# Attention in front of a recurrence and two mixtures: TensorE's groups in another order, PSUM banks allotted anew, key copies placed one by one

## The reference, cut to what matters

```
q = layernorm(x) @ Wq.T + bq         # 16 heads of 16 values
k = ctx @ Wk.T + bk ;  v = ctx @ Wv.T + bv
attn = softmax(q k^T / 4) over the 361 rows of ctx
x = x + tanh(g) * ((attn v) @ Wo.T + bo)
```

## Time and profile before

| | |
|---|---|
| median of three runs | 3206.34 us |
| the profiled execution | 3209.85 us |
| its span, from the first to the last instruction | 3208.1 us |
| busy over the span | PE 90%, DVE 41%, ACT 26%, POOL 25% |
| granted TensorE clock, mean over the span | 0.953 |

### The profile page before, as it was taken

One profiled execution on the slowest core, in us unless ns is written; L12 is line 12 of the kernel. 1 busy time (PEld: TensorE's weight loads), 2 busy tenths in 40 slices (PEclk: granted clock), 3 DMA queues, 4 the chain that ended last, 5 costly groups with the idle time before them and its releaser, 6 DMA issues. The chain is left out here.

```text
span 3208.1 us, 70894 instructions
## 1 busy us (share of the span) xinstructions
PE 2880.4 (90%) x29244; PEld 1559.8 (49%) x29245; DVE 1310.6 (41%) x2655; ACT 827.8 (26%) x2170; POOL 811.1 (25%) x759
## 2 busy tenths in 40 slices
PE   7999999899999999999999999999999974009898
PEld 4566666534444444444444444478566643007555
DVE  5655555613332323323323233264222256986311
ACT  3444444411111111111111111121222246471111
POOL 2111111002222222222222222234444431004243
PEclk9999999999999999999999999999999988559899
DMA  7000100220000000000000000051222263005143
GB/s 239 30 26 26 32 26 26 71 81 23 18 23 18 19 22 18 23 17 21 19 18 25 16 24 16 18 205 47 43 45 45 44 175 98 0 1 206 52 116 75
DMA packets 78391, 164.11 MB, mean 51 GB/s; under 512 B 11788, under 2 KB 51568, under 8 KB 73111
## 3 DMA queue, kind: packets, MB, share of 16 engines
q1 hardware_dynamic: 53588, 104.04, 10.4%
q0 software_dynamic: 21456, 40.57, 5.7%
q10 hardware_dynamic: 3074, 15.45, 1.3%
HBM read 119.63 MB, written 40.37 MB: 50 GB/s over the span
## 5 line engine op out<-in xcount | busy, mean ns | idle before, releaser
L1076 PE MATMUL gru_ps_rz<-whh,scratch 128*32 128x512 f32 x6400 | 709.3, 595 | 0.0
L871 POOL TENSOR_TENSOR scratch<-scratch 128x1024 f32<-128x1024 f32 (+3 forms) x246 | 369.5, 1527 | 818.8 <-DVE stat L885 656.5
L1076 PEld LDWEIGHTS gru_ps_rz<-whh,scratch 128*32 128x32 f32 x6400 | 197.9, 110 | 454.1 <-issue 454.1
L1081 PE MATMUL gru_ps_n<-whh,scratch 128*32 128x256 f32 x6400 | 363.6, 379 | 0.0
L1005 DVE TENSOR_TENSOR scratch<-scratch,state 128x256 f32<-128x256 f32 x100 | 52.2, 522 | 667.4 <-ACT scratch L1034 667.4
L1081 PEld LDWEIGHTS gru_ps_n<-whh,scratch 128*32 128x32 f32 x6400 | 207.7, 110 | 180.2 <-issue 59.9
L467 DVE TENSOR_REDUCE att_neg_max<-att_banks 100x2 f32<-100x722 f32 x256 | 221.1, 906 | 122.6 <-PE att_banks L701 122.6
L1034 ACT ACTIVATE scratch<-gru_ps_rz 128x512 f32<-128x512 f32 x100 | 59.7, 597 | 726.7 <-PE gru_ps_rz L1076 726.7
L390 ACT ACTIVATE att_probsT<-att_banks 121x600 f32<-121x600 f32 x256 | 154.3, 672 | 216.7 <-PE att_banks L744 216.7
L1053 PE MATMUL gru_ps_rz<-wih,scratch 128*32 128x512 f32 x1600 | 191.7, 597 | 1.7 <-POOL scratch L973 1.7
L2392 PE MATMUL e_ps_g<-align_reach,ident 32*121 32x101 f32 x64 | 10.9, 326 | 197.0 <-DVE align_reach L2198 195.5
(11 more groups left out here) (400 smaller groups left out, 4237.8 us busy)
## 6 DMA issues: line engine op xcount, KB each, us to landing
table<-in_w SPq DMA_DIRECT2D x16, 1024.0 KB, 6.9
states<-state SPq DMA_DIRECT2D x100, 128.0 KB
scratch<-states SPq DMA_DIRECT2D x25, 512.0 KB, 3.5
whh<-in_whhT POOLq DMA_DIRECT2D x8, 1536.0 KB, 19.9
att_c_in<-in_ctxT SPq DMA_DIRECT2D x32, 363.0 KB, 3.2
dist_ctx<-in_ctxT SPq DMA_DIRECT2D x32, 363.0 KB, 4.6
align_ctx<-in_ctx_rows SPq DMA_DIRECT2D x32, 363.0 KB
whh<-in_guT ACTq DMA_DIRECT2D x8, 1024.0 KB, 12.3
```

The source lines that it names most:

```text
L871: done = nc.gpsimd.tensor_tensor(last.prod[:, row:row + rows, :], a, b, ALU.mult)
L1076: last = nc.tensor.matmul(ps_rz[quarter(q), :], stateT[c % 2][:, quarter(c // 2)], rz_columns(whh, c, q), start=False, stop=(c == GC - 1))
L1081: last = nc.tensor.matmul(ps_n[quarter(q), 0:GQ], stateT[c % 2][:, quarter(c // 2)], n_columns(whh, c, q), start=(c == 0), stop=(c == GC - 1))
```

## The change

The change alters the order of the calls on TensorE, ScalarE and VectorE, gives each tensor other PSUM banks and rewrites the waits that guard them. `keys_out` copies one half at a time, so that its calls can stand apart. The instructions themselves and their count stay. Shown are the bank tables, the three loops and the waits that the prediction speaks of.

```diff
-        SCORES = ((4, 0), (6, 4), (4, 2), (4, 0))
-        TURNED = ((0, 2), (6, 2), (4, 0), (2, 0))
-        OUTPUTS, XT, QUERIES, BACK, ATT, Y, MAXIMA = 6, 7, 0, 6, 1, 2, 5
-        KEYS, VALUES, V_ORDER = (7, 3), (7, 7, 3), (0, 2, 1)
+        SCORES = ((4, 6), (4, 1), (2, 0), (1, 6))
+        TURNED = ((2, 0), (6, 2), (1, 6), (2, 0))
+        OUTPUTS, XT, QUERIES, BACK, ATT, Y, MAXIMA = 4, 4, 5, 3, 4, 4, 7
+        KEYS, VALUES, V_ORDER = (0, 3), (1, 6, 5), (0, 2, 1)
...
             for i in range(-3, B + 1):          # ScalarE
+                here, after, later, before = valid(i), valid(i + 1), valid(i + 2), valid(i - 1)
-                if valid(i): exponential(i, 0, 0), exponential(i, 0, 1)
-                if i % 2 and valid(i + 3): xnT_out((i + 3) // 2)
-                if valid(i - 1): att_out(i - 1)
+                if before: att_out(i - 1)
                 if i == B: roots(EARLY, B - 1, 2)
-                if valid(i + 1): keys_out(i + 1, 1)
-                if valid(i + 3): queries_out(i + 3)
-                if valid(i): exponential(i, 1, 0), (i, 1, 1), (i, 2, 0), (i, 2, 1)
-                if valid(i - 1): attnT_out(i - 1)
-                if valid(i + 2): keys_out(i + 2, 0)
+                if here: exponential(i, 0, 0), exponential(i, 0, 1)
+                if after: keys_out(i + 1, 1, 0), keys_out(i + 1, 1, 1)
+                if later: keys_out(i + 2, 0, 0)
+                if here: exponential(i, 1, 1), exponential(i, 1, 0)
+                if i % 2 and valid(i + 3): xnT_out((i + 3) // 2)
+                if later: keys_out(i + 2, 0, 1)
+                if here: exponential(i, 2, 0)
+                if valid(i + 3): queries_out(i + 3)
+                if before: attnT_out(i - 1)
+                if here: exponential(i, 2, 1)
                 if i == AT_ROOT: input_roots()
                 if i == EARLY + 1: roots(0, EARLY, 1)
-                if valid(i): exponential(i, 3, 1), exponential(i, 3, 0)
+                if here: exponential(i, 3, 0), exponential(i, 3, 1)
...
             for i in range(-3, B):              # VectorE
+                early_output(i, 0)
+                if 0 <= i < AT_ROOT: input_statistics(i, 0)
                 if after: maxima(i + 1, 0, 0), maxima(i + 1, 0, 1)
-                if after: maxima(i + 1, 1, 0), maxima(i + 1, 1, 1)
-                early_output(i, 0)
-                if 0 <= i < AT_ROOT: input_statistics(i, 0)
+                if after: maxima(i + 1, 1, 1), maxima(i + 1, 1, 0), values_out(i + 1, 0)
                 if before: divide(i - 1)
-                if after: maxima(i + 1, 2, 1), maxima(i + 1, 2, 0)
+                if after: maxima(i + 1, 2, 0), maxima(i + 1, 2, 1)
+                if before: add_output(i - 1)
                 if 0 <= i < AT_ROOT: input_statistics(i, 1)
-                if after: values_out(i + 1, 0), maxima(i + 1, 3, 0), maxima(i + 1, 3, 1)
-                if before: add_output(i - 1)
-                if after: values_out(i + 1, 2), take_maxima(i + 1)
-                if before: statistics(i - 1), aggregate(i - 1)
+                if after: maxima(i + 1, 3, 0), maxima(i + 1, 3, 1), values_out(i + 1, 2)
+                if before: statistics(i - 1), aggregate(i - 1)
+                if after: take_maxima(i + 1)
...
             for i in range(-3, B + 1):          # TensorE
+                if before: outputs(i - 1, 3)
                 if here: scores_less_maxima(i, 0)
-                if before: outputs(i - 1, 3)
-                if i % 2 and valid(i + 3): turn_x((i + 3) // 2)
                 if after: scores(i + 1, 0), project_keys(i + 1, 1), scores(i + 1, 1)
-                if valid(i + 3): project_queries(i + 3)
-                if here: scores_less_maxima(i, 1), scores_less_maxima(i, 2)
-                if before: turn_back(i - 1)
                 if later: project_keys(i + 2, 0)
+                if here: scores_less_maxima(i, 1)
+                if after: project_values(i + 1, 0)
+                if i % 2 and valid(i + 3): turn_x((i + 3) // 2)
+                if before: turn_back(i - 1)
+                if here: scores_less_maxima(i, 2)
+                if valid(i + 3): project_queries(i + 3)
+                if before: turn_attn(i - 1)
                 if after: scores(i + 1, 2)
-                if before: turn_attn(i - 1)
+                if before: project_output(i - 1)
+                if after: project_values(i + 1, 2), scores(i + 1, 3)
                 if here: outputs(i, 0), outputs(i, 1), scores_less_maxima(i, 3)
-                if after: project_values(i + 1, 0), scores(i + 1, 3)
-                if before: project_output(i - 1)
+                if after: project_values(i + 1, 1), turn_maxima(i + 1)
                 if here: outputs(i, 2)
-                if after: project_values(i + 1, 2), turn_maxima(i + 1), project_values(i + 1, 1)
...
             def project_keys(b, g):
                 if g == 0:
                     pe.wait_ge(ctx_arrived[b % 2], 16 * (b // 2) + 16)
+                    at_least(pe, p_ready[1], HG * (b - 2) + 1)
                 else:
-                    at_least(pe, p_ready[1], HG * (b - 1) + 1)
+                    at_least(pe, p_ready[0], HG * (b - 1) + 1)
...
             def scores(b, c):
                 if c == 0:
+                    at_least(pe, v_ready, 3 * b)
                     at_least(pe, less_ready, 2 * b)
-                    at_least(pe, p_ready[0], HG * (b - 1) + 1)
+                    at_least(pe, att_ready, b - 1)
                 if c == 2:
                     pe.wait_ge(k_ready[1], 2 * b + 2)
+                    at_least(pe, p_ready[0], HG * (b - 1) + 3)
+                    at_least(pe, attn_ready, b - 1)
+                    if b + 1 < B: pe.wait_ge(k_ready[0], 2 * b + 4)
                 if c == 3:
-                    pe.wait_ge(max_ready[0], HG * b + 3)
-                    at_least(pe, p_ready[1], HG * b)
+                    for h in range(2): pe.wait_ge(max_ready[h], HG * b + 3)
+                    at_least(pe, p_ready[1], HG * (b - 1) + 3)
...
             def scores_less_maxima(b, c):
                 if c == 2:
+                    for h in range(2): pe.wait_ge(p_ready[h], HG * b + 2)
+                    if after: pe.wait_ge(v_ready, 3 * b + 4)
```

More of the change, by code:

```diff
@@ L423, in _ @@
                     roots(EARLY, B - 1, 2)
-                if valid(i + 1):
-                    keys_out(i + 1, 1)
+                if here:
+                    exponential(i, 0, 0)
+                    exponential(i, 0, 1)
+                if after:
+                    keys_out(i + 1, 1, 0)
+                    keys_out(i + 1, 1, 1)
+                if later:
+                    keys_out(i + 2, 0, 0)
+                if here:
+                    exponential(i, 1, 1)
+                    exponential(i, 1, 0)
+                if i % 2 and valid(i + 3):
+                    xnT_out((i + 3) // 2)
+                if later:
+                    keys_out(i + 2, 0, 1)
+                if here:
+                    exponential(i, 2, 0)
                 if valid(i + 3):
                     queries_out(i + 3)
[L428 to L431, removed]
+                if before:
+                    attnT_out(i - 1)
+                if here:
                     exponential(i, 2, 1)
[L433 to L436, removed]
                 if i == AT_ROOT:
@@ L581, in _ @@
                 if after:
+                    maxima(i + 1, 2, 0)
                     maxima(i + 1, 2, 1)
-                    maxima(i + 1, 2, 0)
+                if before:
+                    add_output(i - 1)
                 if 0 <= i < AT_ROOT:
@@ L598, in _ @@
                     aggregate(i - 1)
+                if after:
+                    take_maxima(i + 1)
                 if 0 <= i < AT_ROOT:
@@ L798, in _ @@
                     scores(i + 1, 1)
+                if later:
+                    project_keys(i + 2, 0)
+                if here:
+                    scores_less_maxima(i, 1)
+                if after:
+                    project_values(i + 1, 0)
+                if i % 2 and valid(i + 3):
+                    turn_x((i + 3) // 2)
+                if before:
+                    turn_back(i - 1)
+                if here:
+                    scores_less_maxima(i, 2)
                 if valid(i + 3):
                     project_queries(i + 3)
-                if here:
-                    scores_less_maxima(i, 1)
-                    scores_less_maxima(i, 2)
                 if before:
-                    turn_back(i - 1)
-                if later:
-                    project_keys(i + 2, 0)
+                    turn_attn(i - 1)
                 if after:
@@ L810, in _ @@
                 if before:
-                    turn_attn(i - 1)
+                    project_output(i - 1)
+                if after:
+                    project_values(i + 1, 2)
+                    scores(i + 1, 3)
                 if here:
@@ L816, in _ @@
                 if after:
[L817 to L820 removed]
```

(2 more changed lines are left out.)

130 lines of the change are left out of this document (48 added, 82 removed).

## The result

The changed kernel took 3189.17 us (median of 5, 3185.55 to 3193.61), the kernel before beside it 3204.74 (median of 5): ratio 0.9945, interval 0.9933 to 0.9957, so it is faster by 15.6 us, half a per cent. The profiled executions lie further apart: 3209.85 before, 3189.17 after (spans 3208.1 and 3187.4), 20.7 us: the one of before lies 5.1 above its median, and part of the difference is chance. From the last operation of the attention (on VectorE, 635.81 before, 616.92 after) to the end of the span it is 2572.3 us before and 2570.5 after, and between 2570.5 and 2574.8 in all ten profiles, which have the same code there. The stage itself is the sharper measure: it ends 18.9 us earlier in these two.

What follows compares the result with a forecast made beforehand. TensorE's order and its waits bound the attention loop. Loops 4 to 30 -13.6, loops 0 to 3 0, prologue +1.3 and allowance +1.5 make -10.8 us: 3199.0 profiled, 3195.5 as median, range 3186 to 3204.

Steps and rivals of the forecast that it cites:

- the likeliest case: Whole kernel: the forecast itself, 3195.5 us, with chance 0.72, of which 0.62 beyond the 6.4 us a measurement can tell.
- loops 0 to 3: First four attention loops: 80.2 against 80.33 us, so 0; the lost table wait pays for the longer context wait.
- the prologue: Loop -1, where nothing overlaps: values groups stand before scores 2 and turn_maxima, +1.3 us, between 0 and 2.1.
- loops 4 to 30: Attention loops: 27 times -0.43 us, less 2.0 in loop 25, together -13.6 before the allowance of +1.5.
- the allowance: Loop layout: the old order laid out came 0.05 us a loop short, so the new gets the same, +1.5 in all.
- Joins: TensorE groups of one tiling standing together save 0.13 to 0.17 us each; PE's work falls some 0.31 a loop.
- The rival in which new kinds don't join: TensorE: slm-scores, queries-turn_attn, proj-values, values-turn_back save nothing, 0.66 us a loop, +19, so 3214.6; chance 0.05.
- the price that stood beside it: Joins onto transposes: by the skill page's rule they save some half of 0.15 us, result near 3198; 0.15 was kept.
- Waits: TensorE's loop: old waits go and five of 0.10 to 0.22 us come, a net gain of 0.12 a loop.
- Loop 25: ScalarE's root loads tables twice; behind exp(2,1) these fit in before slm 3, so scores 3's wait goes, -2.0 us.
- The context wait: Loop 1, keys waiting for the load beside the recurrent weights: 4.9 us instead of 1.69, with half clock (1.7) behind it.
- Five waits vanish: Rival: the new order's five remaining waits disappear as latencies are shorter, 0.66 us a loop, -19, so 3176; chance 0.05.

Runs made afterwards that it cites:

- the roots alone: Kernel before the change, with only ScalarE's two root functions and their table loads moved behind exponential 3: 3200.17 us, ratio 0.9978.
- the two with the weights spread: Changed kernel with the eight recurrent-weight loads issued one a loop, in loops 0 to 7 (3184.78 us) or loops 4 to 11 (3187.73 us), not all in loop 0.
- the key copies together: Changed kernel with both copies of a batch's first key groups at the later of their two places on ScalarE: 3190.14 us, ratio to before 0.9950.
- two joins undone: Changed kernel with turn_maxima put between out 2 and out 3 instead of behind values 1: 3199.19 us, ratio to before 0.9976.

## Why the prediction was right

The time was forecast at 3195.5 and came to 3189.17: the likeliest case, with two terms too dear, and with two others that came out near by luck (loops 0 to 3 and the prologue). The ledger, of the profiled executions:

| | forecast | measured |
|---|---|---|
| up to slm 1 of loop 0 | +1.3 | +1.10 |
| loops 0 to 3 | 0 | -1.14 |
| loops 4 to 30 | -12.1 (with the allowance) | -19.87 |
| after that | 0 | -0.8 |
| sum | -10.8 | -20.7 |

- **Joins.** Right. Out 0.14 (0.13 forecast), full-array neighbours 0.15 (0.15 and 0.17); queries with turn_attn take 1.05 (271.01 to 272.06) against an estimated 0.87 and 0.32, so 0.14 in a kind that no row had shown. Only slm 0 with scores 0 saves 0.08 that can be seen (0.82 less 0.77, 0.05, was forecast, the rest under the wait). The rival in which new kinds don't join falls, and so does the price that stood beside it: "TensorE: Matmul & The Clock Gate", Part 3, of the Trainium skill lets a weight load overlap running matmuls only where the row group differs, which gave 3198. Here undoing the join of values with turn_maxima cost 0.15 and not half of it, and turn_maxima's load begins 0.75 behind the first of values (277.61 to 278.36), where behind a lone values the next load begins after 1.06; the measurement decides against the rule here.
- **Waits.** The mechanism was right, the size not; this is the step that was mis-sized. Up to values 0 the laid out loop agrees to 0.03 (scores 0 at 0.74 for 0.77, keys 1 at 1.68 for 1.69, slm 1 at 5.31 for 5.32, values 0 at 6.13 for 6.14), and slm 2 comes at 7.84 for 7.88. Then scores 2 is at 9.74 for 9.84 and scores 3 at 12.47 for 12.73; from there on every group is 0.22 early and nothing else differs (slm 0 at 17.69 for 17.91). I had put about 0.1 on each wait that stands behind the one that ends last. In the rows exp(2,0) ends at 271.81 and scores 2 begins at 272.06, when PE itself is free, past three further waits; the last maximum ends at 274.72 and scores 3 begins 0.07 later. At these two places waits already met cost nothing that shows; no run tests it by an edit. That is 0.2 a loop, 5.4 in 27 loops. (0.02 of the 12.73 is a slip: 12.51 plus 0.2 is 12.71.)
- **The allowance** of 1.5 for the layout was for nothing: the old order's shortfall did not come again.
- **Loop 25.** -2.0 was forecast, and -2.15 came (20.43 before, where odd loops from slm 1 to slm 1 usually took 18.28). The tables do fit between exp(2,1) and slm 3; the run with the roots alone shows that the loads were the cause. Loop 26, 19.00 before where even loops took 18.48, lost another 0.52 that no term had. The loads are not its cause, as it stays at 19.00 in that run: turn_x waited there for rows from VectorE (L632, 0.5 in the view of waits).
- **Loops 0 to 3.** The context wait came where it was said, at 3.44 for 4.9 (landing took 9.1 from the issue at 57.41, not 10.1), with the half clock behind it. The spread of the recurrent weights shows their transfers to be the cause. Beyond that wait and four loops of 17.75, 4.75 are left where I had put 1.7 on the clock and 1.8 on the statistics, in all 3.5. Three things that I had not foreseen stand in it: the second wait on the context (1.07, where no other was forecast), and weight loads that broke off for 0.88 and for 1.55 (last section). So the sum of these loops came out near the forecast because a wait that was too dear paid for terms that were missing.
- **Prologue.** The +1.3 came, as +1.10, but by luck. It was forecast for loop -1, so slm 0 should have come at 40.7; it came at 39.19, against 39.39 before. The 1.10 arises behind it, up to slm 1 (46.44 against 45.34). There PE, which had idled 2.44 ahead of values 1 in loop -1, had half clock (0.50), where the kernel before had full clock (the load, then the windows before and after). No run takes the half clock away, so its share is not shown.

```profile
36.59 1.02 PEld L670 LDWEIGHTS att_banks<-att_wv,att_c_in 128*121 128x121 f32 x4 [2.44 <-DVE att_neg_max L472]
```

```profile
37.00:43.00 6.00, 4.24 (x44) 2.50 (x42) 3.81 (x9) 1.23 (x2) 0.00 (x0) 1.00 0.22 65
37.00:43.00 6.00, 5.48 (x40) 3.45 (x39) 3.05 (x8) 1.23 (x2) 0.00 (x0) 0.50 0.23 65
```

- **Five waits vanish** (3176): two of the five did. Those for the copy of att, for exp(0,0) and for the copy of the values stayed, at about 0.10, 0.14 and 0.18.

## What to carry over

Lay out one period of the bounding engine from lone and joined prices of its groups, and price a wait by when its last releaser ends, not by how many waits stand there. An order that puts neighbours of one tiling together earns 0.13 to 0.17 us a join only where the path is not held by a wait, and it hangs on the other engines' orders: one copy on ScalarE two exponentials later turned -16 us into +67. Judge a few tenths of a per cent by the end of the stage that changed, since the rest of this kernel varies by 4 us between executions; and look at the granted clock there first: it moved that end by 3 to 4 us between these profiles (next section).

## What the runs showed that was not expected

With the copy of att put back, a loop that idles PE for 1.8 us has half clock granted for 3.4 us in 15 loops of 27, which costs about 1.6 us in each such loop on top of the wait's 1.8.

The clock also falls at the end of the stage, where PE's last groups wait for other engines, and not at the same place in each execution. In the changed kernel it is full until 613.79, 3 us before the end; with the matmul between slm 0 and scores 0 it falls 16 us before the end (window of the changed kernel, then of that run):

```profile
600.60:613.70 13.10, 8.29 (x185) 6.03 (x185) 4.13 (x14) 6.64 (x12) 0.54 (x1) 1.00 0.23 74
611.60:621.70 10.10, 8.65 (x135) 6.37 (x134) 2.29 (x8) 2.69 (x5) 0.54 (x1) 0.50 0.29 90
```

From slm 1 of loop 31 to the end it is 16.4 us in the changed kernel and 16.0 in the two with the weights spread, but 19.4 in that run, 19.7 with the key copies together and 20.7 with two joins undone. These 3 to 4 us are in the profiled executions of those runs, and none of the three theories has them; what made the clock fall earlier there stays open.

And TensorE's instructions may come late beside the recurrent weights: in the changed kernel weight loads break off within a group, with no semaphore named (first two stalls, then the DMA queues of the time ahead of the second; columns are packets, MB, share of 16 engines):

```profile
59.93 0.40 PEld L741 LDWEIGHTS att_banks<-att_q_less,att_kT 32*121 32x121 f32 x12 [0.88 <-issue]
...
83.38 0.23 PEld L754 LDWEIGHTS att_banks<-att_probsT,att_v 121*32 121x32 f32 x9 [1.55 <-issue]
```

```profile
q0 software_dynamic: 51, 0.52, 96.1%
q8 instruction: 1, 0.02, 5.3%
```

One packet of instructions lands between 80.7 and 82.0 while the software queue holds 96% of the DMA engines, and the stall ends 1.4 us after it. With the weights one a loop, such stalls of 0.79 and 1.66 stand in loops 0 and 2 (59.57, 96.84). With the weights in loops 4 to 11 there is none in loops 0 to 3, and the one long loop among those (18.56) has one of 0.72 (203.54). Each of the five ends 1.3 to 1.5 us behind the landing of an instruction packet. That fits a late fetch; it was not tested by itself.
